# A conditional transformer block on one core: tokens in two halves through all head groups, half 1 convolved by VectorE, out-projection summed in PSUM over four units

## The chip, the core and the metric

The kernel runs on one core of a Trainium2 chip. TensorE (PE) multiplies from SBUF into PSUM, VectorE (DVE), ScalarE (ACT) and GpSimd (POOL) work element by element, and SyncE (SP) issues the transfers. Each engine runs its own list of instructions in order and waits on semaphores. The metric is the device time of one execution in microseconds (us).

## What is computed

x is 32 sequences of 32 tokens with 256 channels. A causal depthwise convolution is added, whose taps are the rows of `cond` (so it reaches over all 32 lags), and then a transformer block with modulation by `cond` is added.

```python
x = x + conv(x, cond[:, None, :])            # causal, 32 taps, one filter per channel
ada = (cond @ ada_w + ada_b)[:, None, :]     # one row for each of the 32 sequences
shift1, scale1, gate1, shift2, scale2, gate2 = split(ada, 6)
x1 = ln(x) * (1 + scale1) + shift1
q, k, v = (x1 @ qkv_w + qkv_b) in 16 heads of 128
attn = softmax(q k^T / sqrt(128))            # within a sequence of 32 tokens
h = x + gate1 * (attn v @ out_w + out_b)
x2 = ln(h) * (1 + scale2) + shift2
x = x + h + gate2 * (gelu(x2 @ ffn_w1 + ffn_b1) @ ffn_w2 + ffn_b2)
```

## The kernel before

All activations lie transposed, 2 tiles of 128 channels (`CT`) by 1024 tokens. A half is 512 tokens. The 16 heads are taken in 4 groups (hg) of 4, and a *unit* is one half in one group. Units go in the order (group 0, half 0), (group 0, half 1), (group 1, half 0) and so on, 8 in all. I number them U0 to U7.

**Weights.** A group's weights are 8 pieces of 128x512 (2 of q, 2 of k, 2 of v, 2 of the out-projection). SP loads them into `raw`. ACT rounds each to `wh` (`high_parts`, L333), POOL takes the rest to `wl` (`low_parts`, L278). Each product is then three matmuls (high and low parts of weights and activations: L930 to L932, for v L939 to L941). Before, this is done once for a group, so 5 times 8 pieces with those of the feed-forward layer.

**A unit on PE** is 12 banks of projections (q 0 to 3, k 4 to 7, v 8 to 11) in three PSUM banks that ACT empties (`evac`), the scores (L992), and, mixed in, the four heads of the unit before: `attend` (L1006) and `out_proj`. DVE does the softmax: `softmax_front` (maximum L617 and difference L619, straight from the bank of scores), then ACT the exponential (L417), then DVE sums and scales (L627 to L631) and transposes (L642). DVE also takes the low part of the attention output (`o_low`, L653) and adds each unit's out-projection to `yacc` (`add_y`, L664 and L668).

**The start.** Tokens come in three chunks: 0 and 1 of 256 tokens (half 0) and 2 of 512 (half 1). Each is convolved partly on PE (a matmul with a diagonal matrix for each lag, L853) and partly on DVE (one multiply-add for each lag and channel tile, L537), the two are added (L547), and a layer norm follows: `mean` on PE (L863), `centre` on DVE (L553), squares on ACT (L371), `var` on PE (L874, for 512 tokens L879), the power -1/2 on POOL (L284), `spread` on PE (L891), norm and shift on DVE, high and low part of x1 (`x1_high` L376, `x1_low` L595). The diagonals are made by ACT (L342) and POOL (L270), 16 each. U0 runs by chunks (`project_chunk`); its chunk 1 and chunk 2's share of the convolution lie between.

**The end.** For each half: `residual` (L743, L747), a second layer norm, `ffn1` with gelu on ACT (L496, L499), low parts on DVE and POOL (L781, L305), `ffn2`, the sum, transposes (L1133), store. The second norm of half 0 lies before and behind the last scores, among other work; that of half 1 among the ffn1 banks of half 0.

The order of every engine's work is written out by hand; nothing is scheduled by a planner.

## Time and profile before

| | us |
|---|---|
| median of 3 runs | 336.99 (336.85 to 337.38) |
| span of the profiled execution | 337.2 |
| PE busy | 319.7 |
| DVE busy | 180.0 |
| ACT busy | 152.7 |
| POOL busy | 80.8 |

The span is from the first to the last instruction of one profiled execution, and it is within 0.2 us of the median. Busy time is the sum of all stretches in which an engine had an instruction under way. PE also has a granted clock: 1.00 is 2.4 GHz, 0.50 is 1.2 GHz. Busy time at the lower clock counts as busy like any other, so the busy share alone does not show it.

### The profile page before, as it was taken

The page shows a single profiled execution, that of the slowest core. Times are in us where ns is not written, and L with a number is a line of the kernel's source. Part 1 is how long each engine was busy: PE and PEld are TensorE (multiplying, and loading weights), DVE is VectorE, ACT ScalarE, POOL GpSimd, SP SyncE. Part 2 cuts the span into 40 slices and gives each one's busy share as a digit, 9 for nine tenths or more (in the row PEclk, how much of TensorE's full clock was granted, in tenths as well). Part 3 has the DMA queues.
Part 4 walks back from the last instruction along what each step waited for, and adds up shares of the span by engine and source line. Part 5 has one row for each costly group of instructions (what it writes and reads, how often), then busy time and mean ns, then how long its engine had stood idle before and what let it go on. Part 6 is the DMA issues. An engine that isn't in the chain of part 4 may idle for free.

```text
span 337.2 us, 6425 instructions
## 1 busy us (share of the span) xinstructions
PE 319.7 (95%) x2655; PEld 269.0 (80%) x2655; DVE 180.0 (53%) x354; ACT 152.7 (45%) x269; POOL 80.8 (24%) x78
## 2 busy tenths in 40 slices
PE   5969599999999999999999999999999999899994
PEld 4959496868888888888888888888898778588884
DVE  4959979866606224333441532631625699783232
ACT  6421032423366525526625535653443557742910
POOL 5606510031034103006303003500201444430400
PEclk9959789999999999999999999999999999999998
DMA  7822100010004202002300101210200000000011
GB/s 247 318 68 62 62 3 0 2 65 0 0 2 126 64 0 64 0 2 68 122 0 0 62 0 41 86 63 0 64 2 0 3 2 0 0 2 0 0 64 62
DMA packets 9607, 14.56 MB, mean 43 GB/s; under 512 B 520, under 2 KB 5744, under 8 KB 9584
## 3 DMA queue, kind: packets, MB, share of 16 engines
q1 hardware_dynamic: 9536, 14.19, 12.9%
q8 instruction: 17, 0.28, 0.3%
q14 instruction: 6, 0.05, 0.1%
q10 hardware_dynamic: 48, 0.03, 0.0%
HBM read 13.18 MB, written 1.05 MB: 42 GB/s over the span
## 4 chain that ended last, share of the span: by engine, by line
PE 79%; DVE 17%; issue 1%; DMA 1%; ACT 1%; DVEq 0%
PE bank L930 16%; PE bank L931 16%; PE bank L932 16%; PE bank L1006 7%; DVE xc L537 6%; PE bank L939 4%; PE bank L941 4%; PE bank L940 4%; PE bank L863 3%; PE bank L992 3%; PE bank L853 3%; DVE pt L642 2%; DVE yacc L747 1%; DVE xc L547 1%; DMA crow<-in_cond_dram 1%
## 5 line engine op out<-in xcount | busy, mean ns | idle before, releaser
L278 POOL TENSOR_TENSOR wl<-raw,wh 128x512 fp32r<-128x512 f32 x40 | 53.1, 1349 | 181.2 <-ACT wh L333 181.2
L930 PE MATMUL bank<-x1h,wl 128*128 128x512 f32 (+1 forms) x176 | 67.8, 385 | 0.0
L931 PE MATMUL bank<-x1l,wh 128*128 128x512 f32 (+1 forms) x176 | 65.9, 374 | 0.0
L932 PE MATMUL bank<-x1h,wh 128*128 128x512 f32 (+1 forms) x176 | 65.8, 374 | 0.0
L394 ACT ACTIVATE pool<-bank,bg 128x512 f32<-128x512 f32 x56 | 38.6, 688 | 57.3 <-PE bank L932 57.0
L653 DVE SCALAR_TENSOR_TENSOR ol<-bank,bT,oh 128x512 fp32r<-128x512 f32 x32 | 23.9, 749 | 46.8 <-ACT oh L423 46.0
L537 DVE SCALAR_TENSOR_TENSOR xc<-x,condT,xc 128x240 f32<-128x240 f32 (+32 forms) x114 | 39.4, 417 | 0.0
L930 PEld LDWEIGHTS bank<-x1h,wl 128*128 128x128 f32 x176 | 34.0, 193 | 6.3 <-issue 0.7
L931 PEld LDWEIGHTS bank<-x1l,wh 128*128 128x128 f32 x176 | 34.0, 193 | 5.8 <-issue 0.2
L932 PEld LDWEIGHTS bank<-x1h,wh 128*128 128x128 f32 x176 | 33.9, 193 | 5.7
L1006 PEld LDWEIGHTS bank<-pt,pool 128*128 128x128 f32 x256 | 31.9, 191 | 3.4 <-issue 0.9
L1006 PE MATMUL bank<-pt,pool 128*128 128x128 f32 x256 | 32.8, 276 | 0.6 <-DVE ol L653 0.4
L423 ACT ACTIVATE oh<-bank,bg 128x512 fp32r<-128x512 f32 x32 | 21.9, 687 | 22.3 <-PE bank L1006 22.3
L617 DVE TENSOR_REDUCE mx<-bank 128x16 f32<-128x512 f32 x8 | 5.5, 691 | 47.2 <-PE bank L992 47.2
L853 PE MATMUL bank<-x,diag 128*128 128x256 f32 (+23 forms) x144 | 30.5, 369 | 0.0
L853 PEld LDWEIGHTS bank<-x,diag 128*128 128x128 f32 x144 | 24.8, 202 | 4.8 <-issue 1.0
L930 PE MATMUL bank<-oh,wl 128*128 128x512 f32 x64 | 26.4, 412 | 0.0
L939 PE MATMUL bank<-wh,x1l 128*128 128x512 f32 x64 | 26.3, 411 | 0.0
L941 PE MATMUL bank<-wh,x1h 128*128 128x512 f32 x64 | 25.0, 391 | 0.0
L932 PE MATMUL bank<-oh,wh 128*128 128x512 f32 x64 | 25.0, 391 | 0.0
L931 PE MATMUL bank<-ol,wh 128*128 128x512 f32 x64 | 25.0, 390 | 0.0
L940 PE MATMUL bank<-wl,x1h 128*128 128x512 f32 x64 | 25.0, 390 | 0.0
(105 smaller groups left out, 450.8 us busy)
## 6 DMA issues: line engine op xcount, KB each, us to landing
raw<-in_L_cond_qkv_w_dram SPq DMA_DIRECT2D x12, 512.0 KB, 3.8
raw<-in_L_cond_out_w_dram SPq DMA_DIRECT2D x4, 512.0 KB, 3.4
raw<-in_L_cond_ffn_w_dram SPq DMA_DIRECT2D x4, 512.0 KB, 3.4
adaw<-in_L_cond_ada_w_dram SPq DMA_DIRECT2D x1, 1024.0 KB, 11.3
out_dram<-pool SPq DMA_DIRECT2D x4, 256.0 KB, 2.2
pool<-in_x_dram SPq DMA_DIRECT2D x2, 256.0 KB, 3.1
adaw<-in_L_cond_ada_w_dram SPq DMA_DIRECT2D x1, 512.0 KB, 5.3
pool<-in_x_dram SPq DMA_DIRECT2D x1, 512.0 KB, 6.1
```

The lines of the kernel that those rows point to most:

```text
L278: g.tensor_tensor(wl[:, cols], raw[:, cols], wh[:, cols].bitcast(F32), ALU.subtract)\
L394: a.activation(dst, src, ACT.Identity, bias=bg[:, j // GH, j % GH:j % GH + 1])\
L537: v.scalar_tensor_tensor(out=acc[:, :, j:], in0=xs[:, :, :T - j], scalar=w, in1=acc[:, :, j:], op0=ALU.mult, op1=ALU.add).then_inc(s_cdve, 1)
L653: v.scalar_tensor_tensor(out=ol[:, h, :], in0=OB[h % 2][:, :], scalar=bT[:, bass.ds(group * GH + (2 * NH + h), 1)], in1=oh[:, h, :].bitcas ...
L853: m = pe.matmul(dst[:, :, j:], diag[:, CT * d + ct, :], xs[:, :, :T - j], start=(i == 0), stop=(i == last))
L930: pe.matmul(dst, wl[:, w_cols], a_hi, start=start, stop=False)
L931: pe.matmul(dst, wh[:, w_cols], a_lo, start=False, stop=False)
L932: return pe.matmul(dst, wh[:, w_cols], a_hi, start=False, stop=stop)
L939: pe.matmul(dst, x1l[:, kt, tk], wh[:, wc], start=(kt == 0), stop=False)
L940: pe.matmul(dst, x1h[:, kt, tk], wl[:, wc], start=False, stop=False)
L941: m = pe.matmul(dst, x1h[:, kt, tk], wh[:, wc], start=False, stop=(kt == CT - 1))
L1006: m = pe.matmul(OB[h % 2][:, t * P:(t + 1) * P], v_sb[:, hn, t, h * P:(h + 1) * P], pt[:, hn, h, t, :], start=True, stop=True)
```

## The change

Units go in another order: half 0 through groups 0 to 3 (U0 to U3), then half 1 through groups 0 to 3 (U4 to U7). What follows from it:

- Each unit needs its group's weights anew: 8 loads, 8 ACT pieces and 8 POOL pieces for every unit, 72 pieces in all in place of 40. The loops over groups are written out.
- The four units of a half add up their out-projection in the two `YB` banks; `add_y` is gone, and `residual` reads the banks.
- Half 1 is not needed before U4. All 32 of its lags are done by DVE (64 instructions), in pieces between the softmaxes of U0 to U2; its layer norm is done in U3. PE convolves lags 16 to 31 of chunks 0 and 1 together (`conv_both`) and lags 6 to 15 of chunk 1 (`conv_second`); DVE does lags 0 to 15 of chunk 0 and 0 to 5 of chunk 1. Diagonals are 26 for each of ACT and POOL.
- The second layer norm of half 0 is done in U5. The attention of U7 is mixed into the first ffn1 banks.
- POOL waits with its weight pieces 2 to 5 of U0 until `x1_low` of chunk 0 is done.

```diff
-    PE_LAGS = [[0] + list(range(6, 17)), [0] + list(range(3, 18)), [0] + list(range(8, 15))]
-    DVE_LAGS = [[j for j in range(1, T) if j not in lags] for lags in PE_LAGS]
+    PE_BOTH = list(range(16, 32))
+    PE_SECOND = list(range(6, 16))
+    DVE_LAGS = [list(range(16)), list(range(6)), list(range(T))]
...
             low_parts(0, range(0, 2))
             rstd(0)
+
+            g.wait_ge(s_lo, CT)
             low_parts(0, range(2, 6))
...
-            with g.Fori(1, NG - 1) as hg:
-                low_parts(hg, range(6, 8))
-                low_parts(hg + 1, range(0, 6))
...
+            for U in range(1, NU):
+                if U == 3:
+                    rstd(2)
+                if U == 5:
+                    rstd(3)
+                low_parts(U, range(6, 8))
+                low_parts(U + 1, range(0, 6))
...
+            high_parts(1, range(0, 6))
+
+            for U in range(1, NU):
+                for j in range(4):
+                    evac(U, j)
+                o_high(U - 1, 0)
+                o_high(U - 1, 1)
+                if U == 3:
+                    squares(2)
...
+                evac(U, 5)
+                high_parts(U, range(6, 8))
+                evac(U, 6)
+                high_parts(U + 1, range(0, 2))
+                evac(U, 7)
...
+                evac(U, 8)
+                high_parts(U + 1, range(2, 4))
+                exps(U)
+                for j in (9, 10, 11):
+                    evac(U, j)
+                high_parts(U + 1, range(4, 6))
...
+            conv(2, 0, 2)
+            modulation(1)
+            modulation(2)
+            one_plus(2, SCALE2)
+            conv(2, 2, 5)
+            softmax_front(0)
+            softmax_probs(0)
...
+            for h in range(GH):
+                o_low(0, h)
+            conv(2, 5, 13)
+            softmax_front(1)
+            softmax_probs(1)
+            softmax_transpose(1)
+            conv(2, 13, 17)
+            for h in range(GH):
+                o_low(1, h)
+            conv(2, 17, T)
+            softmax_front(2)
...
+            for U in range(1, NU):
+
+                ln = {3: 2, 5: 3}.get(U)
+                if U == NG:
+                    pe.wait_ge(s_lo, CT * NC)
+                project(U, range(0, 3))
+                if ln:
+                    pe.wait_ge(s_sd, U)
+                    mean(ln)
+                project(U, (3,))
+                attend(U - 1, 0)
...
+            ffn1(0, (0, 1, 2))
+            attend(last, 0)
+            attend(last, 1)
+            ffn1(0, (3,))
+            attend(last, 2)
+            out_proj(last, 0)
+            attend(last, 3)
+            for h in (1, 2, 3):
+                out_proj(last, h)
+            ffn1(0, (4, 5))
             mean(4)
```

Two places show how the order moves. The first is ACT at the end of U0, before. `wh<-raw` is a piece of a weight's high part, `pexp` the exponential of U0, `pool<-bank` the emptying of a projection bank.

```order
L412 ACTIVATE pool<-bank 128x512 [waits projections]
L417 ACTIVATE pexp<-sd 128x512 [waits scores_less_max]
L412 ACTIVATE pool<-bank 128x512 [waits projections]
L333 ACTIVATE wh<-raw 128x512 [waits raw_o_loaded]
L333 ACTIVATE wh<-raw 128x512
L371 ACTIVATE x<-yacc 128x512 [waits ln_centred] x2
L423 ACTIVATE oh<-bank,bg 128x512 [waits attn_out] x4
L376 ACTIVATE x1h<-yacc 128x512 [waits x1_full] x2
L394 ACTIVATE pool<-bank,bg 128x512 [waits projections] x6
```

The same place after the change, on ACT:

```order
L388 ACTIVATE pool<-bank 128x512 [waits projections]
L392 ACTIVATE pexp<-sd 128x512 [waits scores_less_max]
L388 ACTIVATE pool<-bank 128x512 [waits projections]
L327 ACTIVATE wh<-raw 128x512 [waits projections,raw_q_loaded]
L327 ACTIVATE wh<-raw 128x512
L327 ACTIVATE wh<-raw 128x512 [waits projections,raw_k_loaded]
L327 ACTIVATE wh<-raw 128x512
L327 ACTIVATE wh<-raw 128x512 [waits projections,raw_v_loaded]
L327 ACTIVATE wh<-raw 128x512
L371 ACTIVATE pool<-bank,bT 128x512 [waits projections] x4
```

Behind the last two banks of U0 there now stand the first six weight pieces of U1, with nothing between them and the exponential of U0. Before, U1 used the weights that were there.

The second is DVE in U1 and U2, before: from the low parts of one attention output to the next softmax.

```order
L653 SCALAR_TENSOR_TENSOR ol<-bank,bT,oh 128x512 [waits attn_out_high] x4
L664 COPY yacc<-bank 128x512 [waits out_proj] x2
L617 TENSOR_REDUCE mx<-bank 128x16 [waits scores]
L619 TENSOR_TENSOR sd<-bank,mx 128x512 [waits score_max]
L627 TENSOR_REDUCE sm<-pexp 128x16 [waits exps]
```

And after the change, on DVE in U1 (in U2 the same place holds 30 such instructions, 128x16x15 down to 128x16):

```order
L608 SCALAR_TENSOR_TENSOR ol<-bank,bT,oh 128x512 [waits attn_out_high] x4
L495 SCALAR_TENSOR_TENSOR xc<-x,condT,xc 128x16x27 [waits conv_dve_steps] x2
L495 SCALAR_TENSOR_TENSOR xc<-x,condT,xc 128x16x26 [waits conv_dve_steps] x2
L495 SCALAR_TENSOR_TENSOR xc<-x,condT,xc 128x16x25 [waits conv_dve_steps] x2
L495 SCALAR_TENSOR_TENSOR xc<-x,condT,xc 128x16x24 [waits conv_dve_steps] x2
L495 SCALAR_TENSOR_TENSOR xc<-x,condT,xc 128x16x23 [waits conv_dve_steps] x2
L495 SCALAR_TENSOR_TENSOR xc<-x,condT,xc 128x16x22 [waits conv_dve_steps] x2
L495 SCALAR_TENSOR_TENSOR xc<-x,condT,xc 128x16x21 [waits conv_dve_steps] x2
L495 SCALAR_TENSOR_TENSOR xc<-x,condT,xc 128x16x20 [waits conv_dve_steps] x2
L580 TENSOR_REDUCE mx<-bank 128x16 [waits scores]
L582 TENSOR_TENSOR sd<-bank,mx 128x512 [waits score_max]
```

The two additions to `yacc` have gone, and 16 multiply-adds of the convolution of half 1 stand between the last `o_low` and the softmax.

## Rows read from the trace of the kernel before

**Rows 1.** The page: busy time of each engine, and the chain that ended last

```profile
PE 319.7 (95%) x2655; PEld 269.0 (80%) x2655; DVE 180.0 (53%) x354; ACT 152.7 (45%) x269; POOL 80.8 (24%) x78
PE 79%; DVE 17%; issue 1%; DMA 1%; ACT 1%; DVEq 0%
```

**Rows 2.** Windows: stretch, its length, busy time of PE, PEld, DVE, ACT, POOL, granted clock, DMA

```profile
18.00:20.00 2.00, 0.23 (x1) 0.26 (x2) 1.59 (x8) 0.00 (x0) 0.00 (x0) 0.50 0.65 237
...
44.00:46.00 2.00, 2.00 (x14) 2.00 (x14) 0.53 (x2) 0.84 (x2) 0.00 (x0) 0.70 0.00 0
```

**Rows 3.** Timeline of PE, start: start, length, instruction, idle before and its releaser

```profile
14.90 1.87 PE L899 MATMUL bank<-condT,adaw 128*128 128x32 f32 x16
19.77 2.05 PE L863 MATMUL bank<-xc,ones 128*128 128x256 f32 x4 [3.00 <-DVE xc L547]
...
34.27 0.37 PE L930 MATMUL bank<-x1h,wl 128*128 128x256 f32 x1
39.76 2.04 PE L863 MATMUL bank<-xc,ones 128*128 128x256 f32 x4 [3.83 <-DVE xc L547]
...
51.72 5.59 PE L853 MATMUL bank<-x,diag 128*128 128x512 f32 x16
...
88.77 0.47 PE L930 MATMUL bank<-x1h,wl 128*128 128x512 f32 x1
```

**Rows 4.** Windows: one unit in the middle, columns as in rows 2

```profile
128.20:155.05 26.85, 26.85 (x271) 22.71 (x271) 10.20 (x15) 12.36 (x21) 4.99 (x4) 1.00 0.07 21
```

**Rows 5.** DVE, convolution: one stretch of the timeline, and groups by shape (last: beside POOL's diagonals)

```profile
52.70 11.83 DVE L537 SCALAR_TENSOR_TENSOR xc<-x,condT,xc 128x416 f32<-128x416 f32 x38
...
L537 DVE SCALAR_TENSOR_TENSOR xc<-x,condT,xc 128x416 f32<-128x416 f32 x2 | 1.2, 640 | 0.0
...
L537 DVE SCALAR_TENSOR_TENSOR xc<-x,condT,xc 128x240 f32<-128x240 f32 x2 | 0.8, 457 | 0.0
...
L537 DVE SCALAR_TENSOR_TENSOR xc<-x,condT,xc 128x240 f32<-128x240 f32 x2 | 1.0, 534 | 0.0
```

**Rows 6.** DVE convolution and POOL weight pieces at the same time, 14 to 31 us

```profile
L537 DVE SCALAR_TENSOR_TENSOR xc<-x,condT,xc 128x64 f32<-128x64 f32 x2 | 2.5, 1296 | 0.0
...
13.97 2.50 POOL L278 TENSOR_TENSOR wl<-raw,wh 128x512 fp32r<-128x512 f32 x2 [2.70 <-ACT wh L333]
...
26.53 4.37 DVE L537 SCALAR_TENSOR_TENSOR xc<-x,condT,xc 128x240 f32<-128x240 f32 x4
26.83 3.94 POOL L278 TENSOR_TENSOR wl<-raw,wh 128x512 fp32r<-128x512 f32 x3
```

**Rows 7.** Timelines of DVE, ACT and POOL in the unit of rows 4

```profile
129.40 0.69 DVE L617 TENSOR_REDUCE mx<-bank 128x16 f32<-128x512 f32 x1 [5.98 <-PE bank L992]
...
146.21 0.75 DVE L653 SCALAR_TENSOR_TENSOR ol<-bank,bT,oh 128x512 fp32r<-128x512 f32 x1 [1.52 <-ACT oh L423]
...
131.48 0.62 ACT L417 ACTIVATE pexp<-sd 128x512 f32<-128x512 f32 x1
...
150.94 0.69 ACT L394 ACTIVATE pool<-bank,bg 128x512 f32<-128x512 f32 x1 [4.77 <-PE bank L932]
151.53 1.14 ACT L333 ACTIVATE wh<-raw 128x512 fp32r<-128x512 f32 x2
...
152.23 2.54 POOL L278 TENSOR_TENSOR wl<-raw,wh 128x512 fp32r<-128x512 f32 x2 [21.58 <-ACT wh L333]
```

**Rows 8.** Timelines of PE, DVE and POOL behind the last scores

```profile
269.53 0.64 PE L879 MATMUL bank<-x,ones 128*32 128x128 f32 x16
...
272.26 1.06 PE L891 MATMUL bank<-ident,rs 128*128 128x128 f32 x8
...
288.28 1.95 PE L863 MATMUL bank<-yacc,ones 128*128 128x512 f32 x4 [1.19 <-DVE yacc L747]
...
297.28 0.48 PE L930 MATMUL bank<-hh,wl 128*128 128x512 f32 x1
...
284.66 3.48 DVE L747 TENSOR_TENSOR yacc<-yacc,xc 128x512 f32<-128x512 f32 x2
```

More of the change, by code:

```diff
@@ L318, in _, with high_parts @@
             a.dma_start(crow[:, :], cond).then_inc(s_row[0], 16)
-            def high_parts(hg, pieces):
-                first = isinstance(hg, int) and hg == 0
+            def high_parts(U, pieces):
                 for p in pieces:
@@ L727, in _, with o_low @@
-            one_plus(2, SCALE2)
-            softmax_front(0, 1)
-            softmax_back(0, 1)
-            unit(1, 0, first_y=True)
-            unit(1, 1)
-            with v.Fori(2, NG - 1) as hg:
-                unit(hg, 0)
-                unit(hg, 1)
-            unit(NG - 1, 0)
+            def o_low(U, h):
+                v.wait_ge(s_ohi, GH * U + h + 1)
+                row = B_V + GH * (U % NG) + h
+                v.scalar_tensor_tensor(out=ol[:, h, :], in0=OB[h % 2][:, :], scalar=bT[:, row:row + 1],
+                                       in1=oh[:, h, :].bitcast(F32), op0=ALU.add, op1=ALU.subtract)\
+                    .then_inc(s_olo, 1)
@@ new lines, in _ @@
+            var_eps(0)
+            conv(1, 2, 4)
+            norm(0)
+            shift(0)
+            x1_low(0)
+            conv(1, 4, len(DVE_LAGS[1]))
+            conv_sum(1)
+            centre(1)
+            scale_up(1)
+            var_eps(1)
+            norm(1)
+            shift(1)
+            x1_low(1)
+            v.wait_ge(s_xe[2], CT)
+            conv(2, 0, 2)
[4 more added lines that the diff above has]
+            softmax_front(0)
@@ L760, in _ @@
+            o_low(2, 0)
+            o_low(2, 1)
+            scale_up(2)
+            var_eps(2)
+            o_low(2, 2)
+            o_low(2, 3)
+            norm(2)
+            shift(2)
+            x1_low(2)
+            softmax_front(3)
+            softmax_probs(3)
+            softmax_transpose(3)
+            for h in range(GH):
+                o_low(3, h)
             residual(0)
-            softmax_front(NG - 1, 1)
+            softmax_front(4)
+            softmax_probs(4)
+            softmax_transpose(4)
@@ L774, in _ @@
             x1_low(3)
-            add_y(NG, -1)
-            residual(1)
+            softmax_front(5)
+            softmax_probs(5)
+            softmax_transpose(5)
+            for h in range(GH):
+                o_low(5, h)
+            residual_sum(0)
+            softmax_front(6)
+            softmax_probs(6)
+            softmax_transpose(6)
+            for h in range(GH):
+                o_low(6, h)
+            softmax_front(7)
+            softmax_probs(7)
+            softmax_transpose(7, slice(0, 2))
@@ L778, in hidden_low @@
+            softmax_transpose(7, slice(2, GH))
             def hidden_low(n, m):
@@ L1043, in _ @@
+            pe.wait_ge(s_xe[1], 1 + CT)
+            conv_both(0, 8)
+            pe.wait_ge(s_row[1], 16 * 5)
+            pe.transpose(PB[2][:, 0:NBIAS], rows[:, :], ident[0:NBIAS, 0:NBIAS]).then_inc(s_bt, 1)
+            conv_both(8, len(PE_BOTH))
+            pe.wait_ge(s_adaw[0], 16)
+            modulation(0)
+            mean(0)
+            conv_second(0, 3)
+            var(0)
+            conv_second(3, 6)
+            spread(0)
+            conv_second(6, len(PE_SECOND))
             pe.wait_ge(s_lo, CT)
@@ L1075, in _ @@
-            pe.wait_ge(s_lo, CT * 3)
-            pe.wait_ge(s_adat, ADA_STEPS[2])
-            project(0, 1, range(0, 9))
-            scores(0, 1)
-            project(0, 1, (9, 10, 11))
-            with pe.Fori(1, NG - 1) as hg:
-                unit(hg, 0)
-                unit(hg, 1)
-            unit(NG - 1, 0)
-            unit(NG - 1, 1, last=True)
-            attend(NG, -1, 0)
-            attend(NG, -1, 1)
-            pe.wait_ge(s_sd, 2 * NG)
-            spread(3)
-            pe.wait_ge(s_pt, 8 * NG + 4)
@@ L1147, in _ @@
                 ffn2(1, k)
+                if k == 0:
+                    var(4)
+                if k == 2:
+                    spread(4)
             ffn1(1, range(MT))
```

655 lines of the change are left out of this document (273 added, 382 removed).

## The prediction, made before the changed kernel was run

> **What bounds the kernel now.** I read the busy times first: PE is busy 95% of the span and carries 79% of the chain that ended last [rows 1]. Then the units: in the middle one PE is busy for all of its 26.85 us while DVE works 10.2, ACT 12.4 and POOL 5.0 us [rows 4]. So in a unit only PE's own work counts, as long as nobody is late for it. The start is different: DVE convolves a chunk, PE waits for it, and PE's clock falls. PE stands 3.00 us before the mean of chunk 0 and 3.83 us before that of chunk 1 [rows 3], the clock is 0.50 (1.2 GHz) behind the first wait and back at 2.4 GHz only within the stretch around 45 us behind the second [rows 2]. A 256-column mean takes 2.04 us there, a 512-column one 1.95 us at full clock [rows 3, 8]. The start has its second layer norm and the convolution of half 1 until 88.77 us [rows 3], when U1's first projection begins. So I price the change as the PE landmarks of a new start, seven units, and the end, with every place where PE would wait.
>
> **Start, up to the first projection.** DVE's lags of chunk 0 were 40 instructions on 4,240 columns and are 32 on 6,272. From the two shapes of rows 5, a column costs (640-457)/176 = 1.04 ns; the 38 instructions there cover 6,528 columns in 11.83 us, so each has 0.13 us beside its columns. While POOL makes diagonals the 240-column one takes 0.08 us more (534 against 457). POOL makes 26 of them in place of 16, so chunk 0 costs 32 x 0.21 + 6.5 = 13.2 us from 5.4 us on (0.4 before today's start, since ACT takes one of the two copies), and the last two meet POOL's first weight pieces, which adds some 1.6 us (below): the end is near 20.2 in place of 18.87 us, and PE's mean starts at 20.8 (before 19.77). From that mean to the first projection were 14.5 us [rows 3]. In there DVE spent 4.37 us on four instructions beside three POOL pieces, worth 1.5 us alone [rows 5, 6]. POOL's new wait for `x1_low` takes these away (-2.9), and PE has some 0.6 us less of convolution in that stretch: 11.0 us, first projection at **31.8** (34.27). DVE's lags 4 and 5 of chunk 1 then meet the POOL pieces that this wait releases, so the next mean comes after 5.3 us, at 37.1 (39.76), again after about 4 us of idle PE. From there to the end of U0's sixth bank were 12.0 us [rows 3], same order: 49.1. Now transposes (1.0), the two modulations (2 x 1.9, by the first of rows 3), five banks of chunk 1 (7.1) and the scores (1.25) give **62.2** for the scores of U0.
>
> **U0 to U1, a new wait.** U1 can't project before its own q weights are split, and on ACT they stand behind the exponential of U0. From the scores: softmax front and hand-over 1.5, exponential 0.7, the last bank 0.5, first high piece 0.6, two POOL pieces 2 x 1.3 [rows 7], and 0.4 because DVE's scaling of the probabilities meets POOL. That is 6.3 us, U1 starts at **68.5**. PE has only one bank (1.4 us) to cover it, so it is idle for 4.9 us. After 3.83 us of idle the clock fell and 5.4 us of work ran at the lower level [rows 2, 3], so I add 2.5 us of lost work. The loads themselves (0.5 MB each) have nearly a unit of lead and cost nothing here; if that lead were gone, each would cost its landing time.
>
> **DVE's convolution against POOL's pieces.** This is the main term. A 64-column instruction takes 1,296 ns beside POOL pieces, and two of them fill the 2.50 us of two pieces; four instructions fill 4.37 us of three pieces [rows 6]. So while POOL has pieces queued, DVE gets one such instruction for each piece. The Trainium skill says which ones suffer: on its page "GPSIMD Engine Reference", section "1. Specifications", the SBUF interfaces are shared, with contention for VectorE instructions that have two SBUF inputs. By that, `o_low` and the softmax front, which read PSUM, pay nothing. It speaks against this change, which sets 64 such instructions beside 32 more pieces.
>
> In a unit POOL's first piece starts 4.0 us before the scores end (152.23 against scores that ended at 156.25, one unit of 26.85 behind the 129.40 of rows 7) and six pieces follow without a gap, since ACT feeds them faster than 1.3 us. The last `o_low` ends at 146.96 [rows 7], 5.3 us before the first piece. In U1, DVE does 10 of 16 instructions in these 5.3 us (432 columns cost 0.58, 368 cost 0.51). The other 6 go one for each piece, at 1.4 us: the softmax starts 4.5 us behind the scores, where it had started at once [rows 7]. ACT's order has the exponential ahead of the bank that PE needs next; counted from rows 7 (exponential 2.1 us behind the scores, then one bank of 0.6, against three PE banks, 4.1 us), 1.45 us of that are slack. PE waits **3.05** us. In U2, 17 of 30 short ones fit into the 5.3 us, 6 go with the pieces, 7 after them at 0.17: the softmax is 4.9 us late, PE waits **3.4** us. Lags 13 to 16 between softmax and `o_low` (3.3 us) fit into DVE's 4 us of idle, but for 0.15.
>
> The skill's page "VectorE: DVE Perf Modes", section "The TRN2 errata", gives 58 cycles beside the columns for an SBUF instruction, 0.06 us at its 0.96 GHz. The rows show 0.13. By the page, more would be done before POOL begins, and the sum below would be about 2.3 us less.
>
> **Layer norms in U3 and U5.** PE: mean 1.95, var 0.64, spread 1.0 [rows 8] = 3.6 us each. Half 1's `x1_low` reads two SBUF tiles beside POOL pieces, which makes the softmax of U3 and U5 late by 2.4 us, less 1.45 slack: 1.0 each. These 9.2 us are no new work for PE; they come out of the start and the end.
>
> **The double weight work.** ACT has 4.6 us and POOL 10 us a unit, within 26.85; it hides except as above. ACT's bank 7 (needed for the scores) ends some 0.05 us ahead of need with two pairs of pieces before it: I take nothing, at worst 0.3 a unit. `add_y` was hidden (DVE idle 5.98 us behind it, rows 7), so dropping it gains nothing.
>
> **End.** From the end of U7's banks, when var began, to ffn2 were 269.5 to 297.3 [rows 8]. Now: ffn1 of half 0 10.9, attention and out-projection of U7 9.0, mean 1.95, and two waits. ACT has three gelu banks and a table load ahead of `o_high`: 1.05. `residual` of half 1 meets the last POOL pieces, like the 3.48 us for two instructions in rows 8: 1.8. Together 24.8. Behind it come 337.2 - 297.28 = 39.9 plus var and spread, 1.6.
>
> **Sum.** 68.5 + (26.85 + 2.5) + 3.05 + 27.0 + 3.4 = 131.3. U3 31.45, U4 26.85, U5 31.45, U6 and U7 53.7 make 274.8. Then 24.8 and 41.5: 341.1. The two waits of over 3 us are as long as the 3.00 us in which the clock fell at the start [rows 2, 3], but there light work stood ahead of it. Whether 3.05 and 3.4 bring a fall each the rows leave open, at 0 or 2.5; I take one: 343.6. The median lies 0.2 under the span: **343.4 us**.
>
> **Rivals.**
> - *The convolution hides (not slower).* If DVE is not held to one instruction for each piece, because POOL yields to a queue of DVE work, then 16 instructions take 8.3 and 30 take 7.9 us from the last `o_low`, which is within 9.3 us to the scores. Both waits and their clock loss go (-9.0), with 1 to 2 us at the residual and U3: **333**. For it: in the 11.83 us of rows 5 DVE had no trouble, but POOL was silent. Against: rows 6, three times. It decides from about 0.7 us an instruction. 0.15.
> - *Smaller waits.* The clock falls later at the start or not in U1 (-2.5), no fall at 3 us (-2.5), the slack is larger: 335 to 340. 0.2.
> - *More clock loss.* Both waits bring a fall (+2.5), and so do the 3.8 us of 32-column modulations in a row, since 1.87 us of them stood ahead of the first fall [rows 2, 3] (+2.4): **348**. 0.2.
>
> My own case, 340.5 to 346.5, has 0.45.
>
> **How the numbers follow.** The likeliest time is 343.4. The lower end takes in half of the first rival and the smaller waits, 333.5; the upper the clock case, 349. A measurement of this kernel tells 0.2% (0.7 us) from no change. Below 336.3: 0.15 and a quarter of the second case, 0.2. Within: 0.07. Above 337.7: 0.73.
>
> **What would show it.** In the profile after: U1's first 512-column projection near 68.5 with an idle of 4 to 5 us released by POOL's `wl`; convolution instructions of 1.2 to 1.5 us beside POOL pieces in U1 and U2; `mx` of U1 and U2 starting 4 to 5 us behind their scores; PE waits of about 3 us at U2's and U3's start; a granted clock of 0.50 behind the longest; units U4, U6, U7 at 26.85. The prediction is wrong if PE goes from U1 to U3 without waits, or if U4, U6 or U7 are longer than 27.2 us, which would mean that ACT or POOL has become late in every unit.

## The result, and the profile after

The changed kernel takes **345.32 us** (median of four runs, 343.53 to 345.60) against 337.19 us before in the same comparison: a ratio of 1.020, with a 95% interval of 1.017 to 1.023. It is slower, by about 2%. The forecast was 343.4 us. In this and in every later comparison a ratio takes only the runs near a kernel's fastest, a median all of its runs. The profiled run took 345.21 us with a span of 343.4 us, so 1.8 us lie around the span.

The page of the kernel after, the lines that answer to [rows 1], with the row of TensorE's granted clock between them (40 slices of 8.6 us, in tenths of full speed):

```profile
PE 315.9 (92%) x2615; PEld 267.2 (78%) x2615; DVE 185.0 (54%) x319; ACT 168.5 (49%) x305; POOL 128.7 (37%) x120
...
PEclk9969696969999998999999999999999999999999
...
PE 73%; DVE 18%; ACT 5%; issue 2%; POOL 1%; DMA 1%; DVEq 0%; ACTq 0%
```

PE has less work than before (315.9 us against 319.7) and a smaller share of the chain (73% against 79%): what the kernel lost, it lost by waiting and by the clock, whose mean over the span is 0.955 here and was 0.977 before. The clock row shows four deep dips, in the slices from 17, 34, 52 and 69 us, and a shallow one from 129 us. POOL's time has gone up from 80.8 to 128.7 us, since every head group's weights are now split twice (and a piece that is made to stand, as below, counts as busy).

The timeline of PE in the kernel after, at the places of [rows 3] and at each later wait. Columns: start, length, instruction, and in brackets the idle time before it and what ended it:

```profile
21.45 0.77 PE L824 MATMUL bank<-xc,ones 128*128 128x256 f32 x1 [2.34 <-DVE xc L508]
38.34 2.05 PE L824 MATMUL bank<-xc,ones 128*128 128x256 f32 x4 [3.96 <-DVE xc L515]
51.00 4.20 PE L856 MATMUL bank<-condT,adaw 128*128 128x32 f32 x32
64.85 1.30 PE L921 MATMUL bank<-pool 128*32 128x32 f32 x128
72.41 0.80 PE L863 MATMUL bank<-x1h,wl 128*128 128x512 f32 x1 [4.67 <-POOL wl L273]
101.89 0.40 PE L863 MATMUL bank<-x1h,wl 128*128 128x512 f32 x1
133.01 0.77 PE L863 MATMUL bank<-x1h,wl 128*128 128x512 f32 x1 [3.55 <-ACT pool L374]
163.67 0.50 PE L872 MATMUL bank<-wl,x1h 128*128 128x512 f32 x1 [1.88 <-issue]
286.94 0.35 PE L935 MATMUL bank<-pt,pool 128*128 128x128 f32 x1 [1.09 <-DVE ol L608]
297.67 0.67 PE L824 MATMUL bank<-yacc,ones 128*128 128x512 f32 x1 [0.52 <-DVE yacc L622]
```

U1 starts at 72.41, U2 at 101.89 **without any wait**, U3 at 133.01 behind 3.55 us. The windows of the same run (stretch, its length, busy time of PE, granted clock, DMA share, GB/s) show what the clock adds:

```profile
52.00:54.00 2.00, 2.00 (x20) 0.98 0.00 0
54.00:56.00 2.00, 2.00 (x10) 0.50 0.00 0
...
72.00:74.00 2.00, 1.59 (x4) 0.50 0.26 42
76.00:78.00 2.00, 2.00 (x7) 0.55 0.76 245
130.00:135.00 5.00, 1.99 (x5) 0.74 0.38 117
```

The clock falls to 1.2 GHz at three places behind the start: at 54 us, where PE had been busy without a gap, for the last 3 us with the 32-column modulations; within the wait of 4.67 us; and within that of 3.55 us. How long it stays down differs between two executions of the same kernel, as the second table of the next section shows.

The last view is that of DVE and POOL in U1 and U2. It answers to [rows 6]. First their timelines:

```profile
88.41 8.43 DVE L495 SCALAR_TENSOR_TENSOR xc<-x,condT,xc 128x432 f32<-128x432 f32 x16
...
115.81 14.58 DVE L495 SCALAR_TENSOR_TENSOR xc<-x,condT,xc 128x240 f32<-128x240 f32 x30
130.31 0.68 DVE L580 TENSOR_REDUCE mx<-bank 128x16 f32<-128x512 f32 x1
...
93.76 13.68 POOL L273 TENSOR_TENSOR wl<-raw,wh 128x512 fp32r<-128x512 f32 x8 [16.46 <-ACT wh L327]
121.17 8.52 POOL L273 TENSOR_TENSOR wl<-raw,wh 128x512 fp32r<-128x512 f32 x6 [13.73 <-ACT wh L327]
```

Then the groups by shape, in one stretch of U1 (two rows) and one of U2 (one row):

```profile
L273 POOL TENSOR_TENSOR wl<-raw,wh 128x512 fp32r<-128x512 f32 x1 | 4.2, 4219 | 16.5 <-ACT wh L327 16.5
L495 DVE SCALAR_TENSOR_TENSOR xc<-x,condT,xc 128x352 f32<-128x352 f32 (+1 forms) x3 | 1.6, 581 | 0.0
...
L495 DVE SCALAR_TENSOR_TENSOR xc<-x,condT,xc 128x80 f32<-128x80 f32 x2 | 2.8, 1426 | 0.0
```

In U2 an 80-column step takes 1.43 us, one for each POOL piece, as [rows 6] had it. In U1 the opposite happened: POOL's first piece came at 93.76 into the running row, DVE's steps kept their 0.58 us, and it was POOL's piece that stood: it lasted 4.22 us and ended 1.1 us behind the row, about its own time. In the row of 304 columns that follows in U1 (from 105.26 us), which began while a POOL piece was already under way, two steps did take turns (1.03 and 1.56 us). So the kernel itself has long steps in both ways.

### The profile page after: what moved, and what is told of

Its sections match the earlier page's. It is cut to its first block, busy times and chain, and to the rows that moved or that the text cites. A ratio compares the mean times of both kernels' runs of the same rounds, so it can differ in the third digit from the quotient of the medians.

```text
span 343.4 us, 6185 instructions
## 1 busy us (share of the span) xinstructions
PE 315.9 (92%) x2615; PEld 267.2 (78%) x2615; DVE 185.0 (54%) x319; ACT 168.5 (49%) x305; POOL 128.7 (37%) x120
## 3 DMA queue, kind: packets, MB, share of 16 engines
HBM read 21.57 MB, written 1.05 MB: 66 GB/s over the span
## 4 chain that ended last, share of the span: by engine, by line
PE 73%; DVE 18%; ACT 5%; issue 2%; POOL 1%; DMA 1%; DVEq 0%; ACTq 0%
PE bank L863 16%; PE bank L865 15%; PE bank L864 15%; DVE xc L495 11%; PE bank L935 7%; PE bank L871 3%; PE bank L824 3%; PE bank L872 3%; PE bank L873 3%; PE bank L921 2%; PE bank L815 2%; PE bank L856 1%; DVE x1l L561 1%; PE bank L849 1%; ACT wh L327 1%
## 5 line engine op out<-in xcount | busy, mean ns | idle before, releaser
L273 POOL TENSOR_TENSOR wl<-raw,wh 128x512 fp32r<-128x512 f32 x72 | 99.0, 1409 | 137.9 <-ACT wh L327 134.3
L863 PE MATMUL bank<-x1h,wl 128*128 128x512 f32 (+1 forms) x176 | 71.7, 407 | 8.9 <-POOL wl L273 4.7
L371 ACT ACTIVATE pool<-bank,bT 128x512 f32<-128x512 f32 x56 | 38.4, 686 | 61.5 <-PE bank L865 61.5
L864 PE MATMUL bank<-x1l,wh 128*128 128x512 f32 (+1 forms) x176 | 68.5, 389 | 0.0
L865 PE MATMUL bank<-x1h,wh 128*128 128x512 f32 (+1 forms) x176 | 68.4, 389 | 0.0
L495 DVE SCALAR_TENSOR_TENSOR xc<-x,condT,xc 128x240 f32<-128x240 f32 (+38 forms) x102 | 54.5, 608 | 0.1
L608 DVE SCALAR_TENSOR_TENSOR ol<-bank,bT,oh 128x512 fp32r<-128x512 f32 x32 | 23.8, 750 | 48.1 <-ACT oh L396 47.2
L863 PEld LDWEIGHTS bank<-x1h,wl 128*128 128x128 f32 x176 | 36.3, 206 | 16.8 <-POOL wl L273 6.0
L327 ACT ACTIVATE wh<-raw 128x512 fp32r<-128x512 f32 x72 | 41.0, 625 | 3.5 <-PE bank L865 3.5
L396 ACT ACTIVATE oh<-bank,bT 128x512 fp32r<-128x512 f32 x32 | 21.9, 686 | 18.9 <-PE bank L935 18.9
L603 DVE STREAM_TRANSPOSE pt<-pnorm 32x512 f32<-32x512 f32 (+1 forms) x36 | 23.2, 644 | 1.2
```

What stands on the lines that cost most here:

```text
L273: g.tensor_tensor(wl[:, cols], raw[:, cols], wh[:, cols].bitcast(F32), ALU.subtract)\
L327: a.activation(wh[:, cols], raw[:, cols], ACT.Copy).then_inc(s_whi, 1)
L371: a.activation((q_sb if j < GH else k_sb)[:, j % GH, :], src, ACT.Identity, bias=bias(U, j // GH, j % GH)).then_inc(s_ev, 1)
L495: m = v.scalar_tensor_tensor(out=acc[:, :, j:], in0=xs[:, :, :T - j], scalar=w, in1=(acc if i else xs)[:, :, j:], op0=ALU.mult, op1=ALU.add)
L608: v.scalar_tensor_tensor(out=ol[:, h, :], in0=OB[h % 2][:, :], scalar=bT[:, row:row + 1], in1=oh[:, h, :].bitcast(F32), op0=ALU.add, op1=A ...
L863: pe.matmul(dst, wl[:, w_cols], a_hi, start=start, stop=False)
```

## The experiments

Ratios are to the kernel before, run on the same chip. The changed kernel itself, run again among them, gave 346.04 us and 1.019 (1.013 to 1.024).

> The changed kernel itself, for the comparison on the same chip as the others of this set: 345 us, ratio 1.02 to the kernel before.

| kernel | median us | ratio (95%) |
|---|---|---|
| changed kernel again | 346.04 | 1.019 (1.013 to 1.024) |
| early_weights | 338.37 | 0.986 (0.980 to 0.991) |
| mod_spread | 343.81 | 1.012 (1.008 to 1.016) |
| lags_reversed | 348.38 | 1.028 (1.022 to 1.034) |
| conv_earlier | 340.93 | 1.010 (1.007 to 1.013) |
| drop_lags (leaves work out) | 339.67 | 0.998 (0.994 to 1.003) |
| combined | 336.44 | 0.994 (0.991 to 0.996) |
| combined_two | 331.55 | 0.980 (0.975 to 0.985) |

The ten runs of early_weights spread from 331.74 to 340.44 us with mean granted clocks from 0.989 to 0.959, so for it I go by the median, 7.7 us under the changed kernel's. The kernels of this table ran on three chips, on which the kernel before had medians of 338.02, 338.29 and 337.75 us; the changed kernel's own runs, on one of them, spread from 342.39 to 348.45 us. So a difference of 2 us between two rows needs the profile beside it.

The profiles can be compared by stretches of PE's timeline (us; one profile of each kernel, two of the changed one):

| kernel | first modulation at about 51 us to the end of U0's scores | U1's start to U2's | U2's start to U3's |
|---|---|---|---|
| changed kernel, two profiles | 15.15 and 13.64 | 29.48 and 28.58 | 31.12 and 31.13 |
| early_weights | 13.63 | 26.99 | 31.12 |
| mod_spread | 12.09 | 28.86 | 31.14 |
| lags_reversed | 15.15 | 29.52 | 34.62 |
| conv_earlier | 12.11 | 29.26 | 28.90 |
| drop_lags | 13.64 | 28.57 | 27.44 |
| combined | 12.09 | 26.95 | 28.92 |
| combined_two | 12.08 | 28.00 | 26.98 |

The first two stretches differ between the two profiles of one and the same kernel, by 1.5 and 0.9 us: the clock stays down for longer or shorter in them. The third, in which TensorE works at full clock, agrees within 0.02 us wherever the lags are the same.

**The weights of unit 1, split earlier** (ScalarE's order in unit 0):

```diff
                 if j == 8:
                     high_parts(0, range(6, 8))
-            high_parts(1, range(0, 6))
+                if j == 9:
+                    high_parts(1, range(0, 2))
+                if j == 10:
+                    high_parts(1, range(2, 4))
+            high_parts(1, range(4, 6))
```

> ScalarE rounds the first four weight pieces of unit 1 right behind banks 9 and 10 of unit 0 instead of behind the exponentials and the last bank. If TensorE's 4.67 us before unit 1 is nothing but this order, the wait goes, and with it most of the 2.65 us that the half clock after it costs: 345.3 - 4.7 - 2.6 = 338.0 us. Rival: the first attention of unit 0 takes its place, since the softmax is late as well; then 1 to 2 us of wait stand at about 73 us and the clock falls all the same: 341.5 us. Second rival: the clock is at half speed from 54 us anyway and only comes back by then, so only the 4.7 us go: 340.6 us.

338.37 us: the first theory's 338.0. PE's timeline at the start of U1, and the window behind it:

```profile
65.26 0.50 PE L867 MATMUL bank<-x1h,wl 128*128 128x512 f32 x1 [0.94 <-POOL wl L273]
...
66.00:68.00 2.00, 2.00 (x10) 1.00 0.80 215
```

The wait went from 4.67 to 0.94 us, and the clock is at full from 64 to 84 us. No wait for the probabilities came in its place. So the wait was ScalarE's order, and the half clock behind it was that wait. By the stretches that clock is worth 1.6 to 2.5 us, and with the 3.7 us of wait 5.3 to 6.2 of the 7.7 us are accounted for.

**The modulations in two lots** (TensorE's order in unit 0):

```diff
-            modulation(1)
-            modulation(2)
             pe.wait_ge(s_lo, CT * 2)
-            project_chunk(1, range(0, 5))
+            modulation(1)
+            project_chunk(1, range(0, 2))
+            modulation(2)
+            project_chunk(1, range(2, 5))
```

> The 32 modulation matmuls of 32 columns (4.2 us in a row at 51.0) are put in two lots of 16, one ahead of the first bank of chunk 1 and one behind its second. Theory C (so long a row of small matmuls brings the clock down): the granted clock stays at full through 52 to 62, and the first banks of chunk 1 no longer run at half: 345.3 - 2.8 = 342.5 us. Rival: the clock fell at 54 because of the idle 3.96 us at 38 or of something else ahead of it; then it falls at about the same time and the time stays within 0.5 us of 345.3. Second rival: each lot of 16 brings it down by itself, 345 to 347 us.

343.81 us, 2.2 us under the changed kernel, with runs (338.94 to 345.17) that overlap with its own. The clock stays at full where it had fallen (columns as above):

```profile
52.00:54.00 2.00, 2.00 (x19) 1.00 0.00 0
54.00:56.00 2.00, 2.00 (x21) 1.00 0.00 0
```

The stretch takes 12.09 us, in all three kernels that have this edit. Without it, it takes 15.15 us in two profiles, 13.6 us in three, and in that of conv_earlier 12.11 us: there the same 32 matmuls ran in a row, and the clock did not fall.

```profile
48.94 3.66 PE L856 MATMUL bank<-condT,adaw 128*128 128x32 f32 x32
...
50.00:52.00 2.00, 2.00 (x21) 1.00 0.00 0
52.00:54.00 2.00, 2.00 (x19) 1.00 0.00 0
```

So a row of such matmuls can bring the clock down but doesn't always: in five profiles of six it did, with the lots apart in none of three. The second rival falls, since no lot of 16 brought it down. Against the first, something else ahead of the fall, stand only these counts. The edit is worth between nothing and 3.1 us in one execution; and the wait ahead of U1 was 5.44 us with it for 4.67.

**The lags in reverse order:**

```diff
-    DVE_LAGS = [list(range(16)), list(range(6)), list(range(T))]
+    DVE_LAGS = [list(range(16)), list(range(6)), [0] + list(range(T - 1, 0, -1))]
```

> The lags of half 1 are taken as 0, 31, 30, .. 1, so the last group (30 steps, behind the fourth o_low of unit 1 at about 116 us) has 272 to 496 columns instead of 16 to 240. Undisturbed that is 30 x (0.13 + 384 / 960) = 15.9 us against 14.58 now. Theory L (long steps hold GpSimd off): it takes 15.9 us, GpSimd has pieces of 4 us there, and the softmax of unit 2 is 1.4 us later than now: 346.7 us, or some 2 us more where GpSimd's weights are late too. Theory O (one step for each piece whatever its length): 6 pieces take 6 steps of 1.4 us, the group takes 21 us, and the time is 351 to 352 us. In unit 1 the group of 80 to 192 columns ends ahead of GpSimd's start and takes 4.4 us instead of 8.43.

348.38 us. The last row took 15.97 us, as theory L had it to a tenth, and POOL's piece beside it stood for 11.75 us; the price is that TensorE now waits for POOL at unit 3 (a group of one stretch, then PE's timeline):

```profile
L273 POOL TENSOR_TENSOR wl<-raw,wh 128x512 fp32r<-128x512 f32 x1 | 11.7, 11747 | 14.8 <-ACT wh L327 14.8
L495 DVE SCALAR_TENSOR_TENSOR xc<-x,condT,xc 128x416 f32<-128x416 f32 x2 | 1.2, 652 | 0.0
...
134.70 0.79 PE L863 MATMUL bank<-x1h,wl 128*128 128x512 f32 x1 [7.63 <-POOL wl L273]
```

This run alone would have made "long steps hold POOL off" look shown.

**The disputed cost by itself.** Three kernels that compute nothing of the reference: DVE does rows of convolution steps of one length, POOL six pieces beside each row. In the first both begin together.

> A kernel of its own that computes nothing of the reference (it stores x back). Twelve stages; in each VectorE does 14 scalar_tensor_tensor steps of the kind of the convolution (two SBUF inputs, 16-batch view) and GpSimd does 6 subtractions of 128x512 beside them. The stages differ in the length of VectorE's step (48, 64, 128, 240, 304, 320, 352, 416 columns, each step waiting for the one two back, then 64, 128, 304, 416 with the wait four back). Theory L (the length decides): steps up to 304 columns are let in once for each GpSimd piece, so those beside GpSimd take about 1.3 to 1.4 us each and GpSimd's pieces stay at 1.40; from 320 columns on VectorE's steps keep their own 0.13 us + columns / 960 MHz (0.46 to 0.56 us) and GpSimd stands, with a piece of 4 us or more, until VectorE's 14 steps are through. Theory G (the gap between two dependent steps decides): with the wait four back even the short steps hold GpSimd off, so 64 and 128 columns take 0.20 and 0.26 us each. Theory O (who came first keeps it): GpSimd and VectorE start together in every stage, and all lengths look alike, about 1.4 us a step while GpSimd works.

The timeline of two of its stages, 128 and 416 columns (DVE, POOL, DVE, POOL), and a stretch of the 416-column one by groups:

```profile
32.72 9.80 DVE L132 SCALAR_TENSOR_TENSOR xc<-x,condT,xc 128x128 f32<-128x128 f32 x14
32.86 7.68 POOL L112 TENSOR_TENSOR wl<-raw,wh 128x512 fp32r<-128x512 f32 x6 [1.73 <-DVE condT L124]
...
92.66 14.01 DVE L132 SCALAR_TENSOR_TENSOR xc<-x,condT,xc 128x416 f32<-128x416 f32 x14
92.80 9.48 POOL L112 TENSOR_TENSOR wl<-raw,wh 128x512 fp32r<-128x512 f32 x6 [4.13 <-DVE condT L124]
...
L132 DVE SCALAR_TENSOR_TENSOR xc<-x,condT,xc 128x416 f32<-128x416 f32 x2 | 3.2, 1646 | 0.0
L112 POOL TENSOR_TENSOR wl<-raw,wh 128x512 fp32r<-128x512 f32 x2 | 3.2, 1606 | 0.0
```

Every length takes turns, 416 columns too: 1.65 us a step where it has 0.65 alone. POOL's piece is longer too, 1.61 us beside 416 columns for 1.26 beside 64. Theory L falls, and theory G with it (64 columns with the wait four back took 8.96 us, as with it two back). The price is the same for all lengths: each POOL piece adds 1.0 us to one DVE step. Theory O is right that lengths look alike, but its figure of 1.4 us holds only for short steps.

The second lets POOL in only after five steps, and varies the dependence.

> As the first probe, but GpSimd's six subtractions are let go only when VectorE has five of its 20 steps behind it. Stages: 416, 304, 240, 176, 128, 96, 64 columns with the wait for the step two back; 64 with it four back; 416, 240, 128 with it one back. In the first probe, where both began together, every step of every length took its turn with one subtraction (416 columns: 1.65 us, 64 columns alike in kind); in the changed kernel a subtraction that came into a running row of 320 to 496 columns stood for the whole row (4.22 us, and 11.75 us with the lags reversed), and one that came at 112 columns got in behind a step of 96. Theory G (a gap between VectorE's steps lets GpSimd in; long steps that are ready leave none): with the wait two back 416, 304, 240 and 176 columns keep their own time (0.56 us for 416), and the first subtraction lasts for the 15 steps left (8 us at 416); 96 and 64 take turns; with the wait one back GpSimd gets in at every length. Theory O (who came first): in all stages GpSimd stands until VectorE's 20 steps are done, 64 columns too. Theory T (turns always): all stages look as in the first probe, and what held GpSimd off in the kernel is something else.

Theory T: all eleven stages take turns (with the wait one back a piece adds 0.9 us to a step). Of the 416-column one, the stretch ahead of POOL's pieces and the one beside them:

```profile
L132 DVE SCALAR_TENSOR_TENSOR xc<-x,condT,xc 128x416 f32<-128x416 f32 x5 | 2.9, 646 | 0.0
...
L132 DVE SCALAR_TENSOR_TENSOR xc<-x,condT,xc 128x416 f32<-128x416 f32 x5 | 7.9, 1647 | 0.0
L112 POOL TENSOR_TENSOR wl<-raw,wh 128x512 fp32r<-128x512 f32 x4 | 6.3, 1608 | 0.0
```

So coming late into a running row is not what gets POOL refused. In both probes POOL was let go by DVE's own semaphore. In the kernel ScalarE lets it go, and the third probe does that, in 14 stages, each with the moment moved by 0.05 us or so.

> As the probes before, VectorE doing 20 steps each waiting for the one two back, but GpSimd's six subtractions are let go by ScalarE, after three copies of which the last grows by 64 columns from stage to stage, so that GpSimd's request falls at eight points of the running step (steps of 416 columns) and at six (128 columns). Theory P (the moment at which GpSimd asks decides, and who is refused once is refused at every step that follows): in some of the 416 stages the first subtraction stands until VectorE's row is over (9 us or so) and the steps keep 0.56 us, in the others it takes turns from the next step on; 128 columns the same. Theory T (turns always): no stage differs from the first probes, and the refusal in the kernel has another cause. Theory A (ScalarE's release instead of VectorE's own is what matters): all stages of 416 columns refuse.

Here the refusal appears, at **128 columns**: of the six stages the first takes turns, the other five refuse (timeline of DVE and POOL in the first two of the six):

```profile
154.84 11.37 DVE L145 SCALAR_TENSOR_TENSOR xc<-x,condT,xc 128x128 f32<-128x128 f32 x20
...
156.58 7.64 POOL L114 TENSOR_TENSOR wl<-raw,wh 128x512 fp32r<-128x512 f32 x6 [7.96 <-ACT act L125]
...
166.34 5.34 DVE L145 SCALAR_TENSOR_TENSOR xc<-x,condT,xc 128x128 f32<-128x128 f32 x20
...
168.15 10.75 POOL L114 TENSOR_TENSOR wl<-raw,wh 128x512 fp32r<-128x512 f32 x6 [3.92 <-ACT act L125]
```

The same 20 steps take 11.37 us in one stage and 5.34 in the next; in the second, POOL's first piece lasts until DVE's row is over. The eight stages of 416 columns all take turns. So none of the three theories holds as it stands, ScalarE's release (A) included. Two things are shown: there are two regimes, turns and refusal, and which one holds is not a matter of the step's length, since 416 columns took turns in the probes and stood POOL off in the reversed kernel, and 128 columns did both. A refusal held to the end of DVE's row in all five of these stages and in every row of the kernels in which a piece was refused by steps of 208 columns and more; in U2 of the changed kernel POOL's first piece stood for four steps of 112 and 96 columns (2.06 us) and then got its turn. What picks the regime stays open. The moment of asking doesn't do it alone: POOL began 97 ns ahead of DVE's next step where it got its turn and 111 ns ahead of it in a stage that refused.

**The lags cut otherwise** (order 0 to 31 as before; the four places are ahead of unit 0's softmax, behind its `o_low`, behind unit 1's softmax and behind its `o_low`):

```diff
-            conv(2, 2, 5)
+            conv(2, 2, 7)
-            conv(2, 5, 13)
+            conv(2, 7, 15)
-            conv(2, 13, 17)
+            conv(2, 15, 19)
-            conv(2, 17, T)
+            conv(2, 19, T)
```

> The same 32 lags of half 1 in the same order, only cut otherwise: 0 to 6 ahead of unit 0's softmax (VectorE sat idle 6.62 us there), 7 to 14 behind o_low of unit 0, 15 to 18 behind unit 1's softmax, 19 to 31 behind o_low of unit 1 (26 steps, 6.4 us undisturbed, from 116 us, so through at about the time at which GpSimd's pieces begin, 121.2). Theory W (the wait of 3.55 us before unit 2's attention is the last row of 30 steps, six of them behind GpSimd's pieces): softmax of unit 2 starts with its scores, the wait and the 1.35 us of half clock after it go, 345.3 - 4.9 = 340.4 us. Rival: GpSimd's pieces come late in unit 1 instead, held off by the longer steps, and the weights of unit 2 or 3 become what TensorE waits for: no gain, 345 us or over. Second rival: the wait goes and the clock falls all the same: 341.8 us.

340.93 us, 5.1 us under the changed kernel, and theory W had said 340.4. The last row still met POOL (12.93 us for 26 steps), and the wait went to 1.91 us, not to nothing:

```profile
109.91 12.93 DVE L495 SCALAR_TENSOR_TENSOR xc<-x,condT,xc 128x208 f32<-128x208 f32 x26
...
125.46 0.47 PE L863 MATMUL bank<-x1h,wl 128*128 128x512 f32 x1 [1.91 <-ACT pool L374]
```

The time came out as theory W had it, the mechanism only in part, so the agreement is luck: from U2 to U3 the profile gained 2.2 us (31.1 to 28.90), and it was 4 to 5 us ahead before U1 had begun (67.30 us for 72.41 and 71.54), where the edit changes nothing that TensorE waits for. Part of that is the clock at 51 us, as told above.

**The last lags left out:**

```diff
-    DVE_LAGS = [list(range(16)), list(range(6)), list(range(T))]
+    DVE_LAGS = [list(range(16)), list(range(6)), list(range(17)) + [T - 1]]
...
-            conv(2, 17, T)
+            conv(2, 17, 18)
```

> Leaves work out: of the last 15 lags of half 1 (17 to 31) only lag 31 is done, so VectorE has 2 steps instead of 30 behind unit 1's o_low. It prices what meets GpSimd in unit 2. Theory W: the wait of 3.55 us and its 1.35 us of half clock go, nothing else: 340.4 us, that is what conv_earlier (340.9) already has but for 1.9 us of wait left there: 339 to 340.5 us. Rival: the wait before unit 2's attention stays in part because ScalarE or the transposes are late too: 342 us or more.

339.67 us (334.89 to 342.13), in the range of theory W, and the wait ahead of U3 is gone: DVE sat idle for 9 us ahead of the softmax.

```profile
113.87 0.40 DVE L495 SCALAR_TENSOR_TENSOR xc<-x,condT,xc 128x16 f32<-128x16 f32 x2
123.27 0.69 DVE L580 TENSOR_REDUCE mx<-bank 128x16 f32<-128x512 f32 x1 [9.00 <-PE bank L921]
```

By the medians the row of 30 steps costs 6.4 us. The profiles show 3.7 us of them up to U3's start (31.1 to 27.44), and behind it 2.8 us at half clock in one profile of the changed kernel and 5.5 us in the other, which costs half of that. They need not be paid: combined_two, below, does all steps and has no wait there.

**All of it together.** Besides the edits of early_weights and mod_spread (with VectorE's part of the modulations behind its first five lags), the first combination cuts the lags as conv_earlier does and moves `x1_low`, in unit 3 as shown and in unit 5 alike:

```diff
-            x1_low(2)
             softmax_front(3)
             softmax_probs(3)
             softmax_transpose(3)
+            x1_low(2)
```

> All of it: the weight pieces of unit 1 rounded behind banks 9 and 10 of unit 0, the modulations in two lots, the lags cut 0-6, 7-14, 15-18, 19-31, and x1_low of the second norm behind the softmax of its unit (units 3 and 5). From the profile of the changed kernel: - 4.7 (wait before unit 1) - 2.6 (its half clock) - 2.8 (half clock from 54 us) - 4.9 (wait before unit 2's attention and its clock) - 1.9 (wait in unit 3) - 0.3 (unit 5): 345.3 - 17.2 = 328 us, and under the kernel before (337 to 338) by 2.5 to 3%. Rival: each wait removed uncovers one of 1 to 2 us behind it (attention of unit 0 for its probabilities, VectorE's o_low late in unit 0): 331 to 333 us.

336.44 us, not 328, and my own edit is the larger part of it. U4's projections start from `x1_low` of half 1, which now came behind the four transposes of the softmax; TensorE waited 4.77 us for it (the rest is a wait of 1.93 us at U3's start, one of 1.42 at U1's, and half clock behind the waits of 4.77 and 1.93):

```profile
160.19 0.79 PE L867 MATMUL bank<-x1h,wl 128*128 128x512 f32 x1 [4.77 <-DVE x1l L565]
```

The second mends this in unit 3 and deals the lags out by length (groups of 13, 8, 3 and 8):

```diff
-    DVE_LAGS = [list(range(16)), list(range(6)), list(range(T))]
+    DVE_LAGS = [list(range(16)), list(range(6)),
+                [0] + list(range(31, 19, -1)) + list(range(1, 8)) + [19] + [16, 17, 18] + list(range(8, 16))]
...
             softmax_front(3)
+            x1_low(2)
             softmax_probs(3)
```

> The combination again with two things mended. In the first one TensorE waited 4.77 us at the start of unit 4 for x1_low of half 1, which I had put behind the whole softmax of unit 3; it now stands between that softmax's subtraction and its sums, where VectorE waits 0.70 us for the exponentials anyway. And the lags are dealt out by length: 0 and 31 to 20 ahead of unit 0's softmax (short ones, through before GpSimd's pieces begin), 1 to 7 and 19 behind o_low of unit 0, 16 to 18 behind unit 1's softmax, 8 to 15 behind o_low of unit 1 (16 steps, 7.5 us, instead of 26 of which 10 met GpSimd). Theory C (each GpSimd piece that meets the row costs one VectorE step 1.03 us, so few long steps are better than many short ones): waits of 4.77 and 1.93 us go and the clock's 0.7 us with the second: 336.4 - 7.4 = 329 us. Rival: x1_low in the middle of the softmax makes attention of unit 3 late by its own 1.3 us and by GpSimd's turns, 1 to 3 us of it reach TensorE: 331 us.

**331.55 us**, 2.0% under the kernel before and 4% under the changed one. The timeline of DVE (first and last row of lags) and of PE at its longest wait behind the start:

```profile
53.69 5.82 DVE L500 SCALAR_TENSOR_TENSOR xc<-x,condT,xc 128x16 f32<-128x16 f32 x24
...
107.51 7.62 DVE L500 SCALAR_TENSOR_TENSOR xc<-x,condT,xc 128x384 f32<-128x384 f32 x16
116.89 0.69 DVE L585 TENSOR_REDUCE mx<-bank 128x16 f32<-128x512 f32 x1 [1.75 <-PE bank L925]
...
150.13 0.58 PE L875 MATMUL bank<-wh,x1l 128*128 128x512 f32 x1 [2.05 <-issue]
```

24 short steps are through before POOL begins, 16 long ones are through before the scores. The wait of U2 to U3 is gone. At U2's start TensorE waited 0.86 us for `wl`, since POOL was refused in U1's row (a piece of 4.92 us). The time is nearer to the rival's 331 us than to 329, but not by the rival's way: no wait for unit 3's attention shows. The wait in U3 (1.88 us in the changed kernel) is still there, 2.05 us. Since in this kernel VectorE does x1_low behind the softmax's subtraction and the wait did not shrink, my reading that x1_low ahead of the softmax made it is not borne out.

The traces point elsewhere. TensorE stops there soon behind the scores, in the changed kernel in the middle of a bank, with no semaphore that would hold it ("issue"). In all nine profiles with the new order (0.89 to 2.44 us; in the kernel before there is no such stop) the DMA queue that the profile calls "instruction" begins a transfer of 16 KB within 1 us of the end of the scores, and TensorE goes on 1.3 to 1.6 us after it has ended. In the changed kernel it runs from 161.31 to 162.24 us, and TensorE goes on at 163.67 (DMA queues in the window 161:163: packets, MB, share):

```profile
q1 hardware_dynamic: 353, 0.35, 52.6%
q8 instruction: 1, 0.02, 2.9%
```

So this wait looks like TensorE waiting for its own code while the DMA engines are busy with weights. No run tests it, and other such transfers, the one at 97.68 us for instance, hold nobody up.

## Why the prediction came out right, point by point

The time was right within 0.6%; several of its terms were not.

- **Start to U0's scores.** Forecast 62.2, measured 66.15. Of the 3.95 us, 1.0 had come by the end of the sixth bank (50.13 for 49.1: the first mean 0.65 late, the second wait 3.96 us as forecast). The rest is the clock's fall at 54 us, put at 2.4 us and 0.2 of chance in the rival "more clock loss". It took place, during 4.20 us of 32-column matmuls in a row, and not in any kernel that has them in two lots. But it is no fixed price: the same work cost 3.1 us of clock in two profiles, 1.5 in three and nothing in one. I had [rows 3] with the same kind of work ahead of the first fall, and took the 3.00 us of idle for its cause alone.
- **U0 to U1.** Forecast 6.3 us and 2.5 of clock; measured 6.26 (66.15 to 72.41) and, by the windows at 0.50 from 72 to 77.7, about 2.65 (0.9 less in the second profile). early_weights shows both as ScalarE's order.
- **U1 to U2.** Forecast a wait of 3.05 us; measured none. This is the step that failed: "the other 6 go one for each piece, at 1.4 us". They took 0.55 to 0.60, and POOL stood. So the overlap of DVE and POOL was wrong here, and the softmax was on time. That is the mechanism of my first rival, in one of its two places. The rule itself, one step for each piece, is what the probes find in all but five of their stages, and U2 has it.
- **U2 to U3.** Forecast 3.4 us; measured 3.55, the softmax 5.2 us late for 4.9. (The prediction's own figures, 5.3 + 6 x 1.4 + 7 x 0.17 - 9.3, give 5.6; 4.9 was a slip that helped.) One fall of the clock was taken for this wait and the one ahead of U2 together; it came here, and cost 1.35 us instead of 2.5, in the second profile 2.8.
- **U3 and U5.** Forecast 1.0 us each for a late softmax; U5 has 0.32 us of it and U3 none that reaches TensorE. The 1.88 us in U3 are the stop for which the code is the likely cause, a term that the prediction doesn't have. U3 took 33.95 us for 31.45, U5 30.84 for 31.45.
- **Units 4, 6, 7.** 26.85 forecast, about 26.9 measured: splitting every group's weights twice is hidden, as the forecast had it.
- **End.** From the end of U7's banks (278.45) to ffn2 23.8 us for 24.8: the wait for `o_high` and `o_low` 1.09 for 1.05, the one ahead of the mean 0.52 for 1.8 (the terms as listed add up to 24.7). From ffn2 (302.21) to the end 41.2 for 41.5.

Against the sum, PE was 3.9 us late at U1's start (72.41 for 68.5), 1.7 at U3's (133.01 for 131.3, the wait of U1 missing), 3.6 at the end of U7's banks (278.45 for 274.8), 2.6 at ffn2 and 2.3 at the end of the span (343.4 for 341.1), which is about the 2.5 us I had added at the end for one more fall of the clock. So a good part of the agreement is offset, not insight. The second profile of the same kernel reaches U1 at 71.54 and U3 at 131.25 us, and its runs spread from 342.39 to 348.45: "a measurement of this kernel tells 0.2%" was too narrow as well.

One term was wrong in another way: "the median lies 0.2 under the span". The span listed with each run is 1.6 to 1.8 us under its time, for the kernel before too (339.14 us with a span of 337.3). The profiled execution of before, with its 337.2 us, was thus one of some 339 us, not one at the median. Span against span, the sum gives 343.6 / 337.2 = 1.019, and 1.020 was measured.

The Trainium skill's page "GPSIMD Engine Reference", section "1. Specifications", says that VectorE instructions with two SBUF inputs contend with GpSimd. The traces agree as to which instructions suffer: beside POOL pieces in U1 the scaling of the probabilities, with two SBUF inputs, took 1.38 us for 0.69, the sums 0.69 as ever. They put about 1.0 us for each 128x512 piece to it. That one of the two can also be kept out for a whole row is shown only by the runs here.

## What to carry to other kernels

Before work is moved to VectorE beside GpSimd, count GpSimd's pieces in the stretch: each costs one two-input VectorE step about 1.0 us whatever its length (48 to 416 columns here), unless it is refused, and then what waits for GpSimd pays. Put such rows where GpSimd is silent, short steps first. A wait is to be priced with the clock behind it, and a stretch of small matmuls with a clock that may fall; such a price is a range, since it changed from one execution to the next. Both can be cured by the order alone: here three changes of order and one of lengths took 14.5 us off the same work.

## What I had not expected of the hardware

- VectorE and GpSimd have two regimes on the same instructions: turns (416 columns 1.65 us, 128 columns 1.35 us a step) or refusal (GpSimd's piece of 1.3 us lasting 4.22, 4.66 and 11.75 us). It comes out the same wherever the same order meets: U1's first piece took 4,219, 4,218 and 4,225 ns in the changed kernel's two profiles and mod_spread's, and 4,219 and 4,214 in those of early_weights and drop_lags.
- TensorE's clock fell while it was busy without a gap, during some 4 us of 32-column matmuls, in five profiles of six, and stayed at full in all three with a bank between two lots of 1.9 us.
- TensorE stopped for 0.89 to 2.44 us in U3 with no semaphore to wait for, and went on 1.3 to 1.6 us after a 16 KB transfer of the queue named "instruction" had ended, in all nine profiles. That the transfer was the cause is not shown.
